# Fourth self-attention: keys, values and queries in banks of their own, two biases on ScalarE, and the spectrum's sums in TensorE's accumulation

## The reference, cut to what matters

```python
q = u @ Wq.T + bq ; k = u @ Wk.T + bk ; v = u @ Wv.T + bv      # u = layernorm(x), 64 x 256
q = dwconv(q, convq_w, convq_b) ; k = dwconv(k, convk_w, convk_b)   # 3 taps, causal
kv = k * v
y = irfft(rfft(kv, n=2*L) * rfft(ssm_kernel, n=2*L))[..., :L]
y = (y + kv * D_skip) * q
return y.T @ Wo.T + bo
```

## Time and profile before

| | us |
|---|---|
| Time before, median of 3 runs | 1074.34 |
| Lowest and highest of the 3 | 1071.56 and 1075.83 |
| The profiled execution's own time | 1074.79 |
| Its span in the trace | 1073.0 |
| Mean granted TensorE clock of the profiled execution | 0.988 |
| TensorE busy | 1005.9 (94% of the span) |
| VectorE busy | 723.2 (67%) |
| ScalarE busy | 364.4 (34%) |

### The profile page before, as it was taken

The page is one execution under the profiler, slowest core; times in us unless marked ns, Lnnn a source line. Parts: engine busy times, 40 slices in busy tenths (PEclk is TensorE's granted clock), DMA queues, the critical chain, the costliest instruction groups (busy, mean ns, idle before and its releaser), DMA issues.

```text
span 1073.0 us, 20778 instructions
## 1 busy us (share of the span) xinstructions
PE 1005.9 (94%) x7863; PEld 658.4 (61%) x7888; DVE 723.2 (67%) x1923; ACT 364.4 (34%) x658; POOL 157.0 (15%) x143
## 2 busy tenths in 40 slices
PE   6999999998789988998999999999999998988988
PEld 4776676765335544365777777676777776843544
DVE  3767767768779835687676767667676767653354
ACT  2332333234327731443333333333333332211204
POOL 0000000001000010243222223222222222000000
PEclk9999999999999999998999999999999999999999
DMA  7101101002229996850000000000000000234420
GB/s 281 41 21 27 33 20 39 20 5 95 98 74 188 183 335 235 306 193 2 1 1 1 1 0 0 0 0 0 0 0 0 1 1 1 79 144 174 186 95 4
DMA packets 69161, 77.33 MB, mean 72 GB/s; under 512 B 52592, under 2 KB 59504, under 8 KB 65648
## 3 DMA queue, kind: packets, MB, share of 16 engines
q1 hardware_dynamic: 68672, 75.93, 22.4%
q10 hardware_dynamic: 432, 0.64, 0.2%
HBM read 63.65 MB, written 0.07 MB: 59 GB/s over the span
## 4 chain that ended last, share of the span: by engine, by line
PE 72%; DVE 11%; issue 7%; ACT 3%; POOL 3%; DMA 3%; SPq 0%; DVEq 0%; POOLq 0%
PE ps L2194 15%; PE ps L2155 12%; PE ps L1479 8%; PE ps L2184 7%; PE ps L1469 4%; PE ps L1490 4%; PE ps L1513 2%; PE ps L1525 2%; POOL x_sum L2718 2%; ACT vals L2015 2%; DMA x_keys<-vals 2%; DVE S L2410 1%; PE ps L504 1%; PE ps L1873 1%; PE ps L2802 1%
## 5 line engine op out<-in xcount | busy, mean ns | idle before, releaser
L2194 PE MATMUL ps<-vals,S 128*128 128x257 f32 x784 | 188.6, 384 | 0.7 <-ACT S L2644 0.7
L2155 PE MATMUL ps<-keysT,row_biases_sb 128*128 128x512 f32 (+1 forms) x416 | 186.4, 574 | 0.1
L2718 POOL TENSOR_TENSOR x_sum<-x_max,consts 128x4 f32<-128x4 f32 (+1 forms) x104 | 133.8, 1287 | 323.7 <-DVE x_max L2398 323.7
L2410 DVE SCALAR_TENSOR_TENSOR S<-ps,x_sum,keysT 128x128 f32<-128x128 f32 x392 | 110.9, 344 | 71.5 <-PE ps L2194 63.0
L2194 PEld LDWEIGHTS ps<-vals,S 128*128 128x128 f32 x784 | 143.4, 192 | 19.0 <-issue 1.0
L2644 ACT ACTIVATE S<-S 128x512 f32<-128x512 f32 (+1 forms) x104 | 62.7, 606 | 219.1 <-DVE S L2445 218.5
L2184 PE MATMUL ps<-x_q,x_keys 128*128 128x128 f32 x784 | 113.9, 287 | 0.0
L2155 PEld LDWEIGHTS ps<-keysT,row_biases_sb 128*128 128x128 f32 x416 | 76.7, 192 | 56.7 <-issue 51.6
L2184 PEld LDWEIGHTS ps<-x_q,x_keys 128*128 128x128 f32 x784 | 96.1, 192 | 0.0
L1479 PE MATMUL ps<-ring,S 128*128 128x512 f32 x196 | 92.2, 593 | 0.7 <-DVE ps L1620 0.7
L504 PE MATMUL ps<-consts 128*128 128x512 bf16 x295 | 75.4, 379 | 4.3 <-issue 0.6
(11 more groups left out here) (453 smaller groups left out, 1391.7 us busy)
## 6 DMA issues: line engine op xcount, KB each, us to landing
ring<-weights SPq DMA_DIRECT2D x24, 1024.0 KB, 5.5
keysT<-ctxT SPq DMA_DIRECT2D x2, 3136.0 KB, 14.6
vals<-ctxN SPq DMA_DIRECT2D x1, 6272.0 KB, 22.7
S<-ctxT SPq DMA_DIRECT2D x12, 512.0 KB, 3.9
keysT<-weights SPq DMA_DIRECT2D x6, 864.0 KB, 8.4
ring<-weights SPq DMA_DIRECT2D x6, 768.0 KB, 7.4
ring<-weights SPq DMA_DIRECT2D x2, 864.0 KB, 5.3
row_biases_sb<-row_biases SPq DMA_DIRECT2D x1, 1416.0 KB, 12.8
```

The lines of the kernel that those rows point to most:

```text
L2155: ins = pe.matmul(ps[:, c % 3, 0:width(c)], x2_wk[:, k, :], ctxT[:, k, span(c)], start=k == 0, stop=k == KT - 1)
L2194: ins = pe.matmul(bank(6, D + 1), S[:, a:a + TILE], ctx_and_ones[:, SUB * c + s, :], start=c == 0 and s == 0, stop=c == NC - 1 and s == su ...
L2410: ins = dve.scalar_tensor_tensor(S[:, a:a + TILE], ps[:, 3 + c % 2, 128 * s:128 * s + 128], x2_inv[:, c % 2, s:s + 1], x2_tile_const, ALU. ...
L2718: pool.tensor_tensor(x2_inv[:, c % 2, 0:n], x2_var[:, c % 2, 0:n], C("neg_half").broadcast_to([128, n]), ALU.pow)\
```

## The change

The projections are made in the order keys, values, queries, into banks 0, 1 and 5, with a signal behind each. VectorE adds the bias of the keys only. ScalarE adds the biases of the values and the queries, with an activation `Identity` that takes the bias as a column, and signals `a3_v_ready` and `a3_q_ready`; VectorE waits for these where it first reads the values and the queries. The fillers are 4 (before: 12), 3 (before: 8) and 3, all in bank 7.

VectorE makes a negated copy of the filter's imaginary part, `a3_negative`, once, behind the copy of the filter. The difference and the sum of the complex product (lines 1257 and 1258) are gone: `a3_left` and `a3_right` hold the four real products, the sign in `a3_negative`, and TensorE accumulates all of them in bank 4, in eight products instead of four. It starts with the four on `a3_left` at `a3_left_ready`, and goes on with `a3_right` at `a3_right_ready`.

```diff
             w = W("a3")
-            for i in range(3):
+            for b, i in ((0, 1), (1, 2), (5, 0)):
                 for o in range(KT):
                     for k in range(KT):
                         a = 512 * i + 256 * k + 128 * o
-                        ins = pe.matmul(ps[:, 0, (2 * i + o) * T:(2 * i + o + 1) * T], w[:, a:a + 128], xnT[:, k, 0, :],
-                                        start=k == 0, stop=k == KT - 1)
-            ins.then_inc(sem("a3_qkv_psum"), 1)
-            busy(pe, 12, 5)
+                        ins = pe.matmul(ps[:, b, o * T:(o + 1) * T], w[:, a:a + 128], xnT[:, k, 0, :], start=k == 0, stop=k == KT - 1)
+                ins.then_inc(sem("a3_qkv_psum"), 1)
+            busy(pe, 4, 7)
             pe.wait_ge(sem("a3_kv_ready"), since("a3_kv_ready", 1))
...
-            busy(pe, 8, 5)
-            pe.wait_ge(sem("a3_product_ready"), since("a3_product_ready", 1))
-            for o in range(KT):
-                for i in range(2):
-                    ins = pe.matmul(ps[:, 4, o * T:(o + 1) * T], a3_left[:, i, 128 * o:128 * o + 128],
-                                    C("idft")[0:FREQ, T * i:T * i + T], start=i == 0, stop=i == 1)
+            busy(pe, 3, 7)
+            pe.wait_ge(sem("a3_left_ready"), since("a3_left_ready", 1))
+            for part, product in enumerate((a3_left, a3_right)):
+                if part == 1:
+                    pe.wait_ge(sem("a3_right_ready"), since("a3_right_ready", 1))
+                for o in range(KT):
+                    for i in range(2):
+                        ins = pe.matmul(ps[:, 4, o * T:(o + 1) * T], product[:, i, 128 * o:128 * o + 128], C("idft")[0:FREQ, T * i:T * i + T],
+                                        start=part == 0 and o == 0 and i == 0, stop=part == 1 and i == 1, skip_group_check=True)
             ins.then_inc(sem("a3_long_psum"), 1)
-            busy(pe, 3, 5)
+            busy(pe, 3, 7)
...
             link(dve, "dve", dve.tensor_copy(a3_filter, cut(ps[0:FREQ, 2, :], 2, D)))
+            link(dve, "dve", dve.tensor_scalar(a3_negative, a3_filter[:, 1, :], -1.0, None, ALU.mult))
             dve.wait_ge(sem("a3_padding"), 1)
             dve.wait_ge(sem("a3_qkv_psum"), since("a3_qkv_psum", 1))
-            for i in (1, 2, 0):
-                for k in range(KT):
-                    out = a3_padded[:, i, k, 2:] if i < 2 else a3_v[:, k, :]
-                    ins = dve.tensor_scalar(out, ps[:, 0, (2 * i + k) * T:(2 * i + k + 1) * T], V("a3_b")[:, 2 * i + k:2 * i + k + 1],
-                                            None, ALU.add)
+            for k in range(KT):
+                ins = dve.tensor_scalar(a3_padded[:, 1, k, 2:], ps[:, 0, k * T:(k + 1) * T], V("a3_b")[:, 2 + k:3 + k], None, ALU.add)
             link(dve, "dve", ins)
             for i in (1, 0):
+                if i == 0:
+                    dve.wait_ge(sem("a3_q_ready"), since("a3_q_ready", 1))
...
                 if i == 1:
+                    dve.wait_ge(sem("a3_v_ready"), since("a3_v_ready", 1))
                     dve.tensor_tensor(a3_kv, a3_conv[:, 1, :, :], a3_v, ALU.mult).then_inc(sem("a3_kv_ready"), 1)
...
-            dve.tensor_tensor(a3_left, spectrum, spread(a3_filter[:, 0, :], 1, 2), ALU.mult).then_inc(sem("a3_part"), 1)
-            dve.tensor_tensor(a3_right[:, 0, :], spectrum[:, 1, :], a3_filter[:, 1, :], ALU.mult).then_inc(sem("a3_part"), 1)
-            dve.tensor_tensor(a3_right[:, 1, :], spectrum[:, 0, :], a3_filter[:, 1, :], ALU.mult).then_inc(sem("a3_part"), 1)
-            dve.wait_ge(sem("a3_part"), 3)
-            link(dve, "dve", dve.tensor_tensor(a3_left[:, 0, :], a3_left[:, 0, :], a3_right[:, 0, :], ALU.subtract))
-            dve.tensor_tensor(a3_left[:, 1, :], a3_left[:, 1, :], a3_right[:, 1, :], ALU.add).then_inc(sem("a3_product_ready"), 1)
+            dve.tensor_tensor(a3_left, spectrum, spread(a3_filter[:, 0, :], 1, 2), ALU.mult).then_inc(sem("a3_left_ready"), 1)
+            dve.tensor_tensor(a3_right[:, 0, :], spectrum[:, 1, :], a3_negative, ALU.mult).then_inc(sem("untold"), 1)
+            dve.tensor_tensor(a3_right[:, 1, :], spectrum[:, 0, :], a3_filter[:, 1, :], ALU.mult).then_inc(sem("a3_right_ready"), 1)
...
         def a3_scalar(act):
             norm_scalar(act, 10)
+            act.wait_ge(sem("a3_padding"), 1)
+            for n, (b, out, bias, done) in enumerate(((1, lambda k: a3_v[:, k, :], 4, "a3_v_ready"),
+                                                      (5, lambda k: a3_padded[:, 0, k, 2:], 0, "a3_q_ready"))):
+                act.wait_ge(sem("a3_qkv_psum"), since("a3_qkv_psum", n + 2))
+                for k in range(KT):
+                    ins = act.activation(out(k), ps[:, b, k * T:(k + 1) * T], ACT.Identity, bias=V("a3_b")[:, bias + k:bias + k + 1])
+                ins.then_inc(sem(done), 1)
             act.wait_ge(sem("a3_kvN_psum"), since("a3_kvN_psum", 1))
```

More of the change, by code:

```diff
@@ L359, in perceiver @@
             "once_ready": (("x2_core_shifted", 6, 1), ("x2_core_probs", 6, 1),
-                           ("f2_attn_ready", 8, 1), ("x3_factor_ready", 9, 1), ("a3_kv_ready", 10, 1), ("a3_product_ready", 10, 1), ("a3_y_ready", 10, 1)),
-            "once_copied": (("x2_mean_ready", 6, 1), ("f2_hT_ready", 8, 1), ("f2_attnT_ready", 8, 1), ("f2_tanh", 8, 1), ("x3_factor_exp", 9, 1), ("a3_kvN_ready", 10, 1)),
+                           ("f2_attn_ready", 8, 1), ("x3_factor_ready", 9, 1), ("a3_kv_ready", 10, 1), ("a3_left_ready", 10, 1), ("a3_right_ready", 10, 1), ("a3_y_ready", 10, 1)),
+            "once_copied": (("x2_mean_ready", 6, 1), ("f2_hT_ready", 8, 1), ("f2_attnT_ready", 8, 1), ("f2_tanh", 8, 1), ("x3_factor_exp", 9, 1), ("a3_v_ready", 10, 1), ("a3_q_ready", 10, 1), ("a3_kvN_ready", 10, 1)),
             "low_ready": (("f1_low_ready", 5, 1), ("f2_mod_ready", 8, 1)),
@@ L364, in perceiver @@
             "queries_psum": (("x0_qT_psum", 0, 1), ("x1_q_psum", 3, 1),
-                             ("x3_qkv_psum", 9, 3), ("a3_qkv_psum", 10, 1)),
+                             ("x3_qkv_psum", 9, 3), ("a3_qkv_psum", 10, 3)),
             "scores_psum": (("x1_scores_psum", 3, PAIRS * PARTS), ("x2_scores_psum", 6, GROUPS * NC),
@@ L1184, in perceiver @@
         a3_filter = cut(scratch(1160, 2 * D, FREQ), 2, D)
+        a3_negative = scratch(2696, D, FREQ)
         a3_left, a3_right = cut(scratch(1672, 2 * D, FREQ), 2, D), cut(scratch(2184, 2 * D, FREQ), 2, D)
```

## The result

| | before | after |
|---|---|---|
| First comparison, median of 8 runs each | 1074.64 us | 1069.95 us |
| Ratio | | 0.9957, 95% interval 0.9941 to 0.9973 |
| The profiled execution's own time | 1074.79 us | 1068.20 us |
| Its span and mean granted clock | 1073.0 us, 0.988 | 1066.4 us, 0.993 |

The kernel became 0.43% faster, 4.6 us by the ratio, where 3.2 us were forecast; the forecast lies in the interval.

The account below looks back on a forecast made before the run. Latency of a serial path through stage 10, no engine full, was taken as the bound. Savings of 2.59 us (first half) and 0.63 us (complex product) sum to 3.22, giving 1071.2 us, range 1068.7 to 1074.5.

Parts of the forecast that it names:

- The path: Stage 10, about 17 us: a serial path between TensorE and VectorE; a microsecond saved should arrive at the end in full.
- Key wait and biases: Stage 10 start: keys first saves 1.82 us, four bias instructions leaving VectorE 0.77; key taps start 2.59 us earlier.
- Values and queries: ScalarE's biases: values ready at least 0.6 us ahead of use; queries about when wanted, 0.1 us delay costing nothing.
- The rival of a late ScalarE: ScalarE biases: an `Identity` table load of 1283 ns makes values late; gain 1.4 us, time 1072.9, chance 0.05.
- Negated copy: VectorE, ahead of the keys' bias: some 0.44 us inside 1.23 us of free time, so it costs nothing.
- Fillers: Ahead of the transposes: four leave TensorE free just in time; cost taken as 0, with 0.09 us kept for the range.
- Complex product: Before the inverse transform: VectorE loses 0.91 us of work, TensorE runs 16 records from the left half; gain 0.63 us.
- Sum: Whole change in stage 10: 2.59 + 0.63 = 3.22 us, 0.3% of the time; 1071.2 us said.
- Clock: Stage 10: granted clock stays 1.00 though 13 fillers go, as they go only where waits go and idle gaps shrink.
- The rival: Clock falls in stage 10 or 11, costing 1.7 us (1072.9) to 3.3 us (1074.4); chance 0.07.

Follow-up runs that it names:

- one signal: Changed kernel, but TensorE starts the inverse transform only when both product halves are ready, 3 fillers ahead: stage 10 16.47 us, 1072.05 us, ratio 0.9994 to before.
- queries first: Changed kernel with projections ordered queries, keys, values, and ScalarE taking queries first: stage 10 14.41 us, 1073.78 us, ratio 1.0005 to before.
- the three later comparisons: The unchanged kernel before, run again beside the experiments on the same chip each time: medians 1072.74, 1073.22 and 1074.68 us.

## Why the prediction was right, point by point

- *The path.* That latency and not a full engine sets stage 10's time held: moving VectorE's start and TensorE's start moved the end one for one, and stage 11 kept its 25.4 us.
- *Key wait and biases.* Forecast 2.59 us to the taps, measured 4.30 - 1.76 = 2.54. VectorE's start came 1.79 us earlier (forecast 1.82). I booked 0.77 us as four instructions leaving VectorE; as a sum that holds, but the experiment with all biases on VectorE shows that two of them needed only a later place.
- *Values and queries.* The values were ready 2.61 us behind the first projection and wanted at 3.36 (forecast 2.51 to 2.71, wanted at 3.32). ScalarE's pair took 0.52 us with no table load. The 0.1 us is in its start, 0.11 us behind the values' last record (an estimate from the stride) where the forecast had 0.03. The rival of a late ScalarE has fallen.
- *Negated copy.* 0.29 us, below the 0.40 of the nearest row, hidden in a wait that still had 0.94 us.
- *Fillers.* Four and three fit. The transposes start 3.71 us behind the first projection record with four fillers and with none, which bears out taking 0 and not 0.09.
- *Complex product.* Forecast 0.63 us, measured 0.69: 16 records in 2.00 us, not 2.05, starting 0.74 us behind VectorE's first product, as worked out (0.75).
- *Sum.* Forecast 3.22 us in the stage, measured 3.23. The runs show 4.7, for the reason that is open above: the forecast had no term for it, and the median of 1069.95 us lies 1.25 us below the 1071.2 that was said, inside the range only because that was wide enough for the scatter. The forecast also held that a comparison tells 0.5% from no change; the intervals here reach some 0.2% to either side, so a gain of 0.43% was told.
- *Clock.* It held, and TensorE was busy for 9.67 us of 10.7 (forecast 9.8 of 10.8). That the shorter gaps are the reason was argued and is not shown: before, with gaps of 0.78 and 0.59 us, the clock held as well. The rival was no idle worry: it set in once the fillers went, and once more when a wait of 0.76 us stood uncovered. The Trainium skill's rule ("TensorE: Matmul & The Clock Gate", the part on the HAM clock gate), that the throttled state is the default and activity releases it, agrees with the trace without fillers, where the clock is 0.53 from 1036 to 1047.

## What to carry to other kernels

On a path that goes back and forth between engines, put a signal behind the smallest piece that the next engine can use, and order the pieces by when they are wanted; that, with the queries' biases moved behind the product, gave 2.0 of the 3.2 us here. The values' biases on an idle engine gave 0.5, and an accumulation that starts on half of its terms 0.7. Removing instructions from an engine pays only where the next engine's start moves with it. Fillers are to be cut to the wait that they cover whenever that wait shortens: too many sit on the path (2.3 us here), too few can let the clock fall (3.7 us here, in one trace and in line with the clocks of its runs).

## What the runs showed that I had not expected

- TensorE's gaps and the clock's falls don't go one to one. In the trace of one signal a fall of some 7 us began 0.6 us behind an uncovered gap of 0.76 us, within the inverse transform. Without fillers a fall of 10 us began 0.8 us into the gap ahead of the transposes. The gap of 0.85 us in queries first came with none in its one trace, nor did those of 0.78 and 0.59 us before.
- Stages 7 and 8 took the same time within 0.02 us in all fourteen traces, and stage 9 one of two values, 37.15 or 38.8 us. Most of the scatter between runs goes with the clock: the standard deviation of before's 97 runs in the three later comparisons is 2.5 us, and 1.5 us are left at equal mean clock. Stage 6, which takes some 520 us, varied most between the traces, from 517.8 to 522.7 us. Single falls were worth 1.6 us (stage 9) to 3.7 us (stage 10 without fillers).
